# Graph convolution on one core: block sums in three PSUM banks, their VectorE additions placed later, the filter bias added by TensorE, row fetches issued half an iteration earlier

## The reference

```python
# two rounds: batch norm, relu, 5 typed linear maps, gather by src, sum by dst
h_new = _round(features, w1, ...); h_new = _round(h_new, w2, ...)
x = _layernorm(x + (h_new + features))
# continuous-filter convolution
h = x @ W_in
W_ij = ssp(f_ij @ Wf1 + bf1) @ Wf2 + bf2      # per edge, ssp = softplus - log 2
W_ij = W_ij * f_ij_cutoff
x_ij = h[idx_j] * W_ij                        # idx_j = dst
out = segment_sum(x_ij, idx_i)                # idx_i = src
y = ssp(out @ Wo1 + bo1) @ Wo2 + bo2
return _layernorm(x + y)
```

## Time and profile before

| | |
|---|---|
| Median of the runs | 7104.06 us |
| Profiled execution, first to last instruction | 7972.1 us |
| Busy share: TensorE, VectorE, ScalarE, GpSimd | 53%, 45%, 16%, 60% |
| First round, second round | 2251.4 us, 2271.2 us |
| Convolution, first 57 iterations | 1432.5 us |
| Convolution, last 41 iterations, with the sums beside them | 1334.5 us |
| Rest of the sums and output stage | 357.5 us |

### The profile page before, as it was taken

The page is one execution under the profiler, slowest core; times in us unless marked ns, Lnnn a source line. Parts: engine busy times, 40 slices in busy tenths (PEclk is TensorE's granted clock), DMA queues, the critical chain, the costliest instruction groups (busy, mean ns, idle before and its releaser), DMA issues.

```text
span 7972.1 us, 70620 instructions
## 1 busy us (share of the span) xinstructions
PE 4199.2 (53%) x19591; PEld 3367.2 (42%) x19591; DVE 3622.4 (45%) x7445; ACT 1295.5 (16%) x3301; POOL 4782.9 (60%) x4809
## 2 busy tenths in 40 slices
PE   6433333333336333333333336566565788788898
PEld 3333333333334323333332334444444566666686
DVE  6322322222326545545544555344333455555578
ACT  2000000000002000000000003444444333333303
POOL 3666666666663777777776665666666544444413
PEclk8555555555557555555556777677777777777799
DMA  6111111111115111111112223222222344444486
GB/s 240 45 46 46 46 46 46 46 47 46 46 45 184 46 46 46 46 46 46 46 46 62 80 76 85 87 92 89 89 91 87 119 144 142 140 140 142 143 264 216
DMA packets 407046, 714.53 MB, mean 90 GB/s; under 512 B 103887, under 2 KB 180850, under 8 KB 405940
## 3 DMA queue, kind: packets, MB, share of 16 engines
q1 hardware_dynamic: 255766, 387.96, 15.4%
q0 software_dynamic: 150912, 322.24, 14.1%
HBM read 509.88 MB, written 199.90 MB: 89 GB/s over the span
## 4 chain that ended last, share of the span: by engine, by line
another core or an unknown queue 38%; PE 19%; DVE 13%; issue 12%; POOL 8%; DMA 4%; ACT 3%; SPq 2%; DVEq 1%; POOLq 0%; ACTq 0%
PE banks L1503 6%; PE banks L1492 4%; POOL edge_rows L519 4%; PE banks L1521 3%; POOL buf_a L519 3%; DMA buf_a<-sorted_rows 2%; PE banks L1381 2%; PE banks L1407 2%; PE banks L1548 1%; DVE work L864 1%; DVE work L827 1%; DVE work L853 1%; DVE onehot L819 1%; ACT buf_a L651 1%
## 5 line engine op out<-in xcount | busy, mean ns | idle before, releaser
L519 POOL DMA_INDIRECT edge_rows<-messages,idx_stage x1568 | 1547.6, 987 | 933.2 <-issue 471.6
L1407 PE MATMUL banks<-onehot,edge_rows 128*128 128x128 f32 x3136 | 790.1, 413 | 1241.4 <-DMA edge_rows<-messages,idx_stage 762.1
L1407 PEld LDWEIGHTS banks<-onehot,edge_rows 128*128 128x128 f32 x3136 | 679.0, 307 | 1360.5 <-DMA edge_rows<-messages,idx_stage 831.2
L562 POOL DMA_INDIRECT sorted_rows<-edge_rows,idx_stage x784 | 792.0, 1010 | 622.2 <-DVE edge_rows L1249 399.2
L562 POOL DMA_INDIRECT sorted_rows<-buf_a,idx_stage x784 | 792.5, 1011 | 610.1 <-DVE buf_a L1249 369.9
L519 POOL DMA_INDIRECT buf_a<-messages,idx_stage x784 | 793.2, 1012 | 333.0 <-issue 233.7
L519 POOL DMA_INDIRECT buf_x<-messages,idx_stage x784 | 750.7, 958 | 375.6 <-issue 242.5
L1503 PE MATMUL banks<-work,buf_a 128*128 128x128 f32 x4744 | 725.0, 312 | 277.8 <-DVE buf_x L1205 242.4
L1503 PEld LDWEIGHTS banks<-work,buf_a 128*128 128x128 f32 x4744 | 662.3, 220 | 416.7 <-DVE work L1190 238.3
L938 DVE TENSOR_TENSOR buf_a<-buf_a,banks 128x128 f32 x392 | 112.5, 287 | 1588.5 <-remote 1464.8
L1407 PE MATMUL banks<-x_onehot,buf_x 128*128 128x128 f32 x1568 | 429.7, 426 | 734.8 <-DMA buf_x<-messages,idx_stage 373.5
(11 more groups left out here) (163 smaller groups left out, 5501.3 us busy)
## 6 DMA issues: line engine op xcount, KB each, us to landing
buf_a<-sorted_rows SPq DMA_DIRECT2D x593, 288.0 KB
messages<-work SPq DMA_DIRECT2D x196, 320.0 KB, 2.2
buf_a<-dst_rows SPq DMA_DIRECT2D x198, 256.0 KB
buf_a<-in_attr SPq DMA_DIRECT2D x198, 128.0 KB
buf_a<-h_in SPq DMA_DIRECT2D x396, 64.0 KB
edge_rows<-messages,idx_stage POOLq DMA_INDIRECT x1568
buf_x<-messages,idx_stage POOLq DMA_INDIRECT x784
buf_a<-messages,idx_stage POOLq DMA_INDIRECT x784
```

Of the source, the lines that this page charges most:

```text
L519: nc.gpsimd.indirect_dma_start(gathered[p][h][:, t, :], None, source, bass.IndirectOffsetOnAxis(ap=idx_stage[:, h, t:t + 1], axis=0),).the ...
L562: nc.gpsimd.indirect_dma_start(sorted_rows, bass.IndirectOffsetOnAxis(ap=idx_stage[:, 2 * u + h, t:t + 1], axis=0), msg_halves[2 * u + h][ ...
L1407: last = nc.tensor.matmul(ps_sums[slot][j], rows_in_slot[:, j * GROUP_TILES + t, :], hot[:, j * GROUP_TILES + t, :], start=(t == 0), stop= ...
```

## The change

1. `filter_bias` and `biased` go. TensorE adds the bias: before the four tiles of each `ps_w` bank it multiplies three rows of ones with the bias split into three bf16 parts (128 x 512, accumulation opened there), and the tiles accumulate on it. VectorE's bias addition (line 1244) goes, and the message is made straight from `ps_w`.
2. The four sums of a half lie in three banks: the first and third in the old one, the second in `ps_w[1]`, the fourth in `ps_w[0]` (`beside_bank`). The waits change: the second waits for the messages of the half before, the fourth for the first message group of its own half, the second layer into `ps_w[0]` for the half before's fourth addition, into `ps_w[1]` for its own half's second addition; the first and the third wait for the addition of the sum before them in their bank.
3. VectorE's additions come later in its order, and its one-hots are built farther from them.
4. SP issues the fetches of half k + 1 in the turn of half k; the first four are issued ahead of the loop.

```diff
@@ -150,8 +151,6 @@
         ones_rows = sb("ones_rows", [3, P], bf16)
-        filter_bias = sb("filter_bias", [P, D])
-        biased = sb("biased", [P, WIDE])
...
@@ -245,7 +244,8 @@
         ps_steps = [ps_b[2][:, 0:FIRST_STEPS], ps_b[3][:, 0:STEPS_IN[1]]]
-        ps_seg = [ps_b[2][:, 0:P], ps_b[0][:, 0:P], ps_b[1][:, 0:P]]
+        ps_seg = [ps_b[2][:, 0:P], ps_b[0][:, 0:P], ps_b[1][:, 0:P], ps_w[1][:, 0:P], ps_w[0][:, 0:P]]
+        beside_bank = [0, 3, 0, 4]
...
-            sp.dma_start(filter_bias[:, :], dram["bf2"].broadcast_to([P, D])).then_inc(s_const_in, 16)
...
@@ -424,12 +423,12 @@
             def refill(beyond):
-                def refill_step(r, adding):
+                def refill_step(r, adding, last_turn=False):
                     bases = load_bases(r + 1)
                     for h in range(2):
-                        if adding:
-                            load_steps((r - (FIRST_ITERS + 1)) * STEP_SLOTS + 4 * h, 4 * h, 4,
-                                       (r - (FIRST_ITERS + 1)) * STEP_SLOTS + 1)
+                        if adding and not (last_turn and h):
+                            turn = r - (FIRST_ITERS + 1)
+                            load_steps(turn * STEP_SLOTS + 4 * (h + 1), 4 * (1 - h), 4, (turn + h) * STEP_SLOTS + 1)
...
-                for r in turns(sp, FIRST_ITERS + 1, ITERS, beyond):
+                load_steps(0, 0, 4, 1)
+                for r in turns(sp, FIRST_ITERS + 1, ITERS - 1, beyond):
                     refill_step(r, True)
+                refill_step(ITERS - 1, True, True)
...
@@ -1207,50 +1208,53 @@
             def convolution_step(r, u, uses, beyond, adding=False, last_turn=False):
                 for h in range(2):
                     k = r * 2 + h
+                    messages = msg_halves[2 * u + h]
                     if adding:
                         turn = r - (FIRST_ITERS + 1)
                         columns = load_columns(turn * STEP_SLOTS + 4 * h)
 
+                    def onehot_ahead(i):
+                        q = 4 * h + i
+                        if adding and not (last_turn and q >= STEP_SLOTS):
+                            step_onehot(turn * STEP_SLOTS + q, q % STEP_SLOTS, turn * 16 + 16 * (q // STEP_SLOTS + 1))
+
                     def add_step(i):
-                        q = 4 * h + i
-                        n = turn * STEP_SLOTS + q
-                        if not last_turn or q + 2 < STEP_SLOTS:
-                            step_onehot(n + 2, (q + 2) % STEP_SLOTS, turn * 16 + 16 * ((q + 2) // STEP_SLOTS + 1))
-                        add_segment(n, q, columns[i], 0)
+                        if adding:
+                            q = 4 * h + i
+                            add_segment(turn * STEP_SLOTS + q, q, columns[i], beside_bank[i])
+
+                    def message_group(j):
+                        dve.wait_ge(s_hcopy, k * 2 + (j + 1 + SLOT2))
+                        tiles = "p (t n) -> p t n"
+                        nc.vector.tensor_tensor(messages[:, j * GROUP_TILES:(j + 1) * GROUP_TILES, 0:D],
+                                                ps_w[j].rearrange(tiles, t=GROUP_TILES),
+                                                h_edge[:, j, :].rearrange(tiles, t=GROUP_TILES), ALU.mult
+                                                ).then_inc(s_msg, 1)
 
                     spread_half(r + h, 1 - h)
-                    if adding:
-                        add_step(0)
+                    onehot_ahead(2)
+                    onehot_ahead(3)
                     dve.wait_ge(s_hcopy, k * 2 + ((2 + SLOT2) if beyond else SLOT2))
                     stage_cutoff(r + h, 1 - h)
-                    if adding:
-                        add_step(1)
                     if beyond:
                         spread_beyond(r, h)
                     dve.wait_ge(s_cut, k + 4)
-                    messages = msg_halves[2 * u + h]
+                    add_step(0)
+                    onehot_ahead(4)
+                    soft_half(k + 1, 1 - h)
+                    add_step(1)
 
                     if uses is not None:
                         dve.wait_ge(s_scat[2 * u + h], scattered(uses))
                     stage_indices(2, k, 2 * u + h)
                     nc.vector.tensor_copy(messages[:, :, D],
                                           src_idx[:, ds(r * ITER_TILES + h * HALF_TILES, HALF_TILES)]).then_inc(s_tagged, 1)
-                    soft_half(k + 1, 1 - h)
                     dve.wait_ge(s_w, k + 1)
-                    for j in range(2):
-                        dve.wait_ge(s_msg, k * 2 + (j + SLOT2))
-                        tiles = "p (t n) -> p t n"
-                        in_tiles = biased.rearrange(tiles, t=GROUP_TILES)
-                        nc.vector.tensor_tensor(in_tiles, ps_w[j].rearrange(tiles, t=GROUP_TILES),
-                                                filter_bias[:, :].unsqueeze(1).broadcast_to([P, GROUP_TILES, D]),
-                                                ALU.add).then_inc(s_biased, 1)
-                        dve.wait_ge(s_biased, k * 2 + (j + 1))
-                        dve.wait_ge(s_hcopy, k * 2 + (j + 1 + SLOT2))
-                        nc.vector.tensor_tensor(messages[:, j * GROUP_TILES:(j + 1) * GROUP_TILES, 0:D], in_tiles,
-                                                h_edge[:, j, :].rearrange(tiles, t=GROUP_TILES), ALU.mult
-                                                ).then_inc(s_msg, 1)
-                        if adding:
-                            add_step(2 + j)
+                    message_group(0)
+                    message_group(1)
+                    add_step(2)
+                    onehot_ahead(5)
+                    add_step(3)
 
             scale_rows(CHUNKS_IN - 1)
             dve.wait_ge(s_acc[1], GROUPS + SUMS)
...
@@ -1494,11 +1498,11 @@
 
             pe.wait_ge(s_cut, 1)
             filter_in(0, 0, 16)
-            def sum_segment(k, q, bank):
+            def sum_segment(k, q, bank, added=None):
 
                 pe.wait_ge(s_step_hot, k + 1)
-
-                pe.wait_ge(s_added, k + (1 if bank else 2))
+                if added is not None:
+                    pe.wait_ge(s_added, added)
                 for t in range(GROUP_TILES):
                     last = nc.tensor.matmul(ps_seg[bank], rows_in[:, q, t, 0:D], step_hot[q % HOT_SLOTS][:, t, :],
                                             start=(t == 0), stop=(t == GROUP_TILES - 1))
@@ -1509,8 +1513,8 @@
                     k = r * 2 + h
                     filter_in(k + 1, 1 - h, (r + h) * 16 + 16)
                     if adding:
-                        turn = r - (FIRST_ITERS + 1)
-                        sum_segment(turn * STEP_SLOTS + 4 * h, 4 * h, 0)
+                        first = (r - (FIRST_ITERS + 1)) * STEP_SLOTS + 4 * h
+                        sum_segment(first, 4 * h, beside_bank[0], first + (SLOT2 - 1))
                     for j in range(2):
 
                         pe.wait_ge(s_win_in[h], r * 32 + 32)
@@ -1522,7 +1526,9 @@
                                                     h_win[:, h, j, :], start=True, stop=True)
                     last.then_inc(s_hexp, 1)
                     if adding:
-                        sum_segment(turn * STEP_SLOTS + (4 * h + 1), 4 * h + 1, 0)
+
+                        pe.wait_ge(s_msg, k * 2 + SLOT2)
+                        sum_segment(first + 1, 4 * h + 1, beside_bank[1])
                     if beyond:
 
                         with pe.Fori(0, 2) as j:
...
@@ -1544,13 +1552,20 @@
                         pe.wait_ge(s_msg, k * 2 + (j - 1 + SLOT2))
                         if beyond:
                             pe.wait_ge(s_xadd, (k * 2 + 2) * BLOCKS + 1)
+                        if adding:
+
+                            pe.wait_ge(s_added, first + (2 * j + SLOT2))
+                        nc.tensor.matmul(ps_w[j], ones_rows[:, :], bias_rows[:, 0, :].unsqueeze(1).broadcast_to([3, 4, D]),
+                                         start=True, stop=False)
                         for t in range(GROUP_TILES):
                             last = nc.tensor.matmul(ps_w[j][:, t * D:(t + 1) * D], soft_halves[h][:, j, t * P:(t + 1) * P],
-                                                    wf2[:, :], start=True, stop=True)
+                                                    wf2[:, :], start=False, stop=(t == GROUP_TILES - 1))
                     last.then_inc(s_w, 1)
                     if adding:
-                        for j in range(2):
-                            sum_segment(turn * STEP_SLOTS + (4 * h + 2 + j), 4 * h + 2 + j, 0)
+                        sum_segment(first + 2, 4 * h + 2, beside_bank[2], first + (1 + SLOT2))
+
+                        pe.wait_ge(s_msg, k * 2 + (1 + SLOT2))
+                        sum_segment(first + 3, 4 * h + 3, beside_bank[3], first + SLOT2)
```

15 lines of the change are left out of this document (9 added, 6 removed).

## The result

The changed kernel takes 6700.6 us (median of 4 runs, 6696.56 to 6709.68), the kernel before beside it 7101.86. The ratio is 0.9438, with an interval of 0.9419 to 0.9457: 401 us off. But the chips of this study fall into two kinds, and on the second kind, where the median of the kernel before is 7922 to 7977 us, kernels close to the changed one gained nothing. That is told with e1, e9 and e10. The changed kernel itself was timed on the first kind alone, and both traces of the kernel before are from the second.

The account below looks back on a forecast made before the run. GpSimd bounds rounds and first 57 iterations; a TensorE, VectorE, SP ring with a low clock bounds the last 41. There 1273.5 us becomes 861, saving 412.5, less 9.5 is 403: 7104.06 - 403 = 6701, given as 6700, range 6640 to 6890.

Parts of the forecast that it names:

- The stage: Last 41 iterations of the convolution, 82 halves: from 15.53 us a half to 10.5, saving 403 us in all.
- the 9.5 us for a first half at 1.2 GHz: Start of the last 41 iterations: one half with TensorE still at the low clock, 9.5 us taken off the saving.
- The pauses: Surpluses in rounds and convolution, 906.5 us together, claimed to belong to the profiled execution and not to timed runs.
- The sum of stages without them: Whole kernel before: profiled span 7972.1 less pauses of 906.5 gives 7065.6 us, 38.5 below the median.
- the expected span of 7570: Profile of the changed kernel: the same saving on top of the profiled execution's pauses, a span near 7570 us.
- TensorE's half: TensorE's work in a half of the last 41 iterations at 2.4 GHz: 9.55 us, bounds 9.05 to 9.82.
- GpSimd's half: Eight scatters set each half of the last 41 iterations: 10.5 us, lower bound 10.16; chance 0.71.
- The second rival: Last 41 iterations: VectorE locks GpSimd out more, three times the scatter stretch, half 11.4 us, 6775 us; chance 0.05.
- The ring: Last 41 iterations: TensorE, VectorE and SP wait in a circle; three links go, and the 3.13 us gap.
- The first rival: Last 41 iterations: TensorE keeps one long gap a half and the changing clock, half 12.9 us, 6889 us; chance 0.15.
- First 57 iterations: First part of the convolution: the bias on TensorE is hidden by GpSimd's pitch, change 0, length within 1%.

Follow-up runs that it names:

- e1: The kernel before, unchanged, profiled once more on a chip of the second kind: 7978.6 us (one run).
- e9: The changed kernel with each bias matmul issued twice, on a chip of the second kind: 7935.5 us, 1.002 of the kernel before.
- e10: The changed kernel with the spread one-hot as scalar_tensor_tensor and the bias on VectorE in the last 41 iterations only, second kind of chip: 7910.6 us, ratio 0.999.
- e7: The changed kernel with the bias addition back on VectorE and the bias matmuls gone, first kind of chip: 6707.5 us, 0.942 of the kernel before.
- e8: The changed kernel with the spread one-hot made by scalar_tensor_tensor in place of tensor_scalar, first kind of chip: 6677.9 us, 0.938 of the kernel before.

## Why the prediction was right, point by point

**The total.** Forecast 6700, measured 6700.6. The saving was worked out as 403 and is 401. The stage was forecast at 82 x 10.5 + 9.5 = 870 and is 852. The kernel before needs 7101.86 - (6700.6 - 852.3) = 1254 us for it, if the other stages are equal, 15.3 a half and not 15.53. (If the first 57 iterations gained the 8 to 10 us told below, it is 1244 to 1246; e7 gives 1259.5 on its chip. So it is 15.2 to 15.4 a half.) The misses of about 19 us on both sides cancel, so the hit to a microsecond is luck; each side by itself is right to 20 or 30. Half of the miss on the new stage is the 9.5 us for a first half at 1.2 GHz: that half was granted the full clock (1.00 from 5499.60 to 5510.00), TensorE having risen before the stage began.

**The pauses.** The sum of stages without them was right as a whole (7065.6 against 7101.86), less so in its parts: of the changed kernel's rounds the first lasts 1978 us, as summed (1975.7), the second 2032, 56 more, and the first 57 iterations 1178.7 against 1158.2. The reason was wrong. I took them for a thing of the profiled execution, but they belong to the chip that it ran on; on such a chip they are in every run. So the expected span of 7570 was wrong as well: it is 6707.8, since that profile is from a chip of the first kind.

**TensorE's half.** This term was mis-sized: 9.55 with bounds of 9.05 to 9.82, measured 10.44. From the half above: a bias matmul and its surroundings cost 0.51 each (5907.20 to 5910.90 is 3.70; the same stretch without them in e7, 5907.81 to 5910.49, is 2.68, which leaves 1.02 for two), twice what I took, and above the 0.385 that I had called an upper bound. The price of an instruction of another shape and type in a stream is not its record's length but the shift of what follows. A further 0.37 is lost where sums and first layer meet (1.00 from 5904.41 to 5905.41 in place of 0.89, 2.04 for two sums in place of 1.78), and the first of the two stands in the trace of before as well, behind the half's first sum of the earlier trace rows (its spread starts 1.00 after it, at 6808.66), but I priced all sums by the 0.89 of another one. The error did no harm because GpSimd is at 10.4 too. That a little more of TensorE's work would have shown is likely from this, but not tested: e9 was meant for it.

**GpSimd's half.** Taken at 10.5 with 10.16 as the lower end; measured 10.39 (852.3 us for 82). The stretch of scatters is 0.14 to 0.22 us a half (8 times 0.984 or 0.994 less 0.967). The Trainium skill (SBUF — State Buffer, Who interferes with whom) puts it down to VectorE's two-port forms such as tensor_scalar. e8 agrees: with another form it is gone in full. The second rival's triple stretch doesn't occur. One reading was wrong: the prediction found no scatter row long enough for a lock, but went by the means. Single scatters are longer than the means: 1.19 us beside the tensor_scalar at 5903.66 above, and 1.56 in the trace of before, beside a message made from two SBUF tiles and the tensor_scalar behind it:

```profile
5019.38 1.56 POOL L562 DMA_INDIRECT sorted_rows<-buf_a,idx_stage  x1 [3.89 <-DVE buf_a L1249]
```

**The ring.** Right in its links: the wait for additions, 227.4 us before, is gone from the trace, rows aren't waited for, and the softplus, behind which the second addition stands, isn't late. On the first kind of chip e7 shows that order, banks and fetch together are the gain (406 us). How it divides among them is known on the second kind alone, and there only in part: the fetch alone gives 0.9%, order, banks and bias without it cost 4.4%. What the banks alone are worth is open.

**The clock.** The first rival, a low clock that goes on, is ruled out on the first kind of chip: 0.99 granted with TensorE busy 841 of 852 us. The Trainium skill (TensorE: Matmul & The Clock Gate, A second HAM failure mode: psum-queue depth-cycling) tells of a kernel that cycles through PSUM banks, idles briefly between its groups and has its clock swing. Here the groups go through several banks too, but no idle time comes between them and the clock doesn't swing: the trace doesn't agree that the banks alone would bring it.

**First 57 iterations.** Forecast at no change, as the change is hidden by GpSimd's pitch; by e7 the bias on VectorE costs them 8 to 10 us, through longer scatters, so the change gained about that much here. The prediction had no term for GpSimd gaining from VectorE's work that goes.

## What to carry to other kernels

Before pricing a change from a profile whose span is far above the runs, split the surplus by stages at the pitch of the engine that bounds them, and price against the kernel without it; but don't say where the surplus comes from until the unchanged kernel has run beside the profile. When two engines end up level, measure each one's relief by itself: here neither TensorE's lighter half nor GpSimd's brought the stage anything. Price an added matmul by the shift of its successors' starts and not by its own length.

## What the runs showed of the hardware

- Two kinds of chip (two sets of runs on the first, three chips of the second): 7102 to 7114 us and 7922 to 7977 us for the same program. On the second, TensorE takes 1.4 us from one instruction to the next about 600 times in a run (590 in e1), and one bank (0.985 to 0.989) beats kernels with three (1.002 in e9, 0.999 in e10). One bank wasn't timed on the first.
- A bf16 matmul of 3 x 512 between float32 matmuls costs TensorE 0.51 us (this trace against e7), and 0.23 behind its like (e9).
- Scatters beside tensor_scalar on VectorE take up to about 1.2 us in the changed kernel (1.19 at 5903.66) in place of 0.97; beside scalar_tensor_tensor with its second input in PSUM, 0.97 (mean of e8).
- TensorE busy for 841 of 852 us was granted 0.99 of 2.4 GHz.
